# Stores and loads in alternating quarters, with a store semaphore for each quarter of a slot

## The chip, the cores and the metric

One core of a Trainium2 chip runs the kernel. The metric is the device time of one execution in microseconds (us), the median of the runs.

## What is computed

`x` is [2048, 64, 16, 16] in float32: 2048 samples of 64 channels, 16 x 16 pixels. It is group-normalised (32 groups of two channels, so over 512 values), padded by one pixel with a few border pixels copied from elsewhere, and run through three masked 4 x 4 convolutions with stride 2 (each mask keeps five taps). Their outputs go to three of the four parities of the output grid, are masked, and are added to x:

```
def _gn(v, G=32, eps=1e-5): ...            # (v - mean) / sqrt(var + eps) over each group
xp = jnp.pad(x, ((0, 0), (0, 0), (1, 1), (1, 1)))
xp = xp.at[:, :, DST_R, DST_C].set(xp[:, :, SRC_R, SRC_C])
up, left, right = (_conv(xp, w * mask, b) for each)
out[0::2, 0::2], out[1::2, 0::2], out[1::2, 1::2] = up, left, right
return x + out * OUT_MASK                  # xp is made from _gn(x)
```

## The kernel before

The samples are cut into 64 chunks of 32. A chunk is 2 MB: 128 partitions (two samples of 64 channels) by 16 pairs (`G`) by 256 pixels. It lives in one of eight slots (`SLOTS`) of the SBUF tensor `xs`, chunk k in slot k % 8, is normalised from there into `tn`, and has the convolution's results added in place, so that the slot is stored from where it was loaded.

The engines work as follows on chunk k. DVE takes the statistics of chunk k+1 (`bn`, L229, two waits on the load's two halves, `loaded[half][slot]`) between the small steps of chunk k (`moments`, `norms`), then normalises half of the pairs of chunk k (L277). ACT takes the root (L307), moves the four PSUM banks of chunk k-2 to `res` (`evacuate`, L336) and normalises the other half (L313). POOL adds `res` of chunk k-2 onto `xs` (`add`, L401, four banks, each raising `bank_added`) and copies the wrapped border pixels of chunk k (`wrap`, L411, five copies). PE does 240 matmuls a chunk (L459).

SP issues all large transfers, in the order written in its block. It first loads the weights, the four quarters of chunk 0 (L199) and chunks 1 to 6 in halves of 1 MB (L189). Then, for each chunk k and each half, it waits until the chunk's adds are done, issues the store of the half (L193), waits until both halves of chunk k-1, which has the slot of chunk k+7, are stored (L211), and issues the load of that half of chunk k+7 (`AHEAD` is 7):

```
for half in range(2):
    sp.wait_ge(bank_added, NB * (k + 1) if k < NCHUNK - 1 else NB * k + 4 + 2 * half)
    store(k, half)
    if n < NCHUNK:
        if n >= SLOTS:
            sp.wait_ge(stored[n % SLOTS], 32 * (n // SLOTS))
        load(n, half)
```

A slot has one semaphore for its two stores, and a transfer raises its semaphore by 16, so 32 a turn means both halves. The rows of a transfer are 1 KB in DRAM.

Of the kernel before, what the change touches and what calls it, by code (L numbers as in the profile page):

```python
# [16 lines left out]
G = 16  # L17
NCHUNK = B // (2 * G)
SLOTS = 8
# [38 lines left out]
NB = len(BANKS)  # L58
# [3 lines left out]


QUARTER = G // 4
HALF = (slice(0, G // 2), slice(G // 2, G))
AHEAD = 7


# [16 lines left out]
def view(tensor, at, dims, first=0, parts=P):  # L85

    full = tensor[:, ]
    row = full.ap[0][0]
    return bass.AP(full.tensor, full.offset + first * row + at, [[row, parts]] + [list(d) for d in dims])


def hex_conv(nc, x, w_up, b_up, w_left, b_left, w_right, b_right, out):
    ctx = ExitStack()
    with ctx:
        def sb(name, shape, dt):
            return ctx.enter_context(nc.sbuf_tensor(name, shape, dt))

        def sem(name):
            return ctx.enter_context(nc.semaphore(name))

        x_dram = x.rearrange("(n g h) c r q -> n (h c) g (r q)", g=G, h=2)
        out_dram = out.rearrange("(n g h) c r q -> n (h c) g (r q)", g=G, h=2)

        xs = sb("xs", [P, SLOTS, G * PIX], F32)
# [21 lines left out]
        def w_raw(t):  # L126
            at = C * 16 * W_AT[t][1]
            return tn[1][W_AT[t][0]:W_AT[t][0] + C, at:at + C * 16]
# [3 lines left out]
            return tn[1][W_AT[t][0]:W_AT[t][0] + C, at:at + C]  # L132

        loaded = [[sem(f"loaded{s}_{half}") for s in range(SLOTS)] for half in range(2)]
        stored = [sem(f"stored{s}") for s in range(SLOTS)]
        w_loaded = [sem(f"w_loaded{t}") for t in range(3)]
        b_loaded = sem("b_loaded")
        quarter = [sem(f"quarter{n}") for n in range(2)]
        cleared = sem("cleared")
        identity = sem("identity")  # L140
        edges_clear = sem("edges_clear")
# [12 lines left out]
        bank_added = sem("bank_added")  # L154
# [26 lines left out]

        @block.sync
        def _(sp):
            def part(dram, k, pairs):
                return dram[k][:, pairs], xs[:, k % SLOTS, :].rearrange("p (g q) -> p g q", g=G)[:, pairs]

            def load(k, half):
                frm, to = part(x_dram, k, HALF[half])
                sp.dma_start(to, frm).then_inc(loaded[half][k % SLOTS], 16)  # L189

            def store(k, half):
                to, frm = part(out_dram, k, HALF[half])
                sp.dma_start(to, frm).then_inc(stored[k % SLOTS], 16)  # L193

            for t, w in enumerate((w_up, w_left, w_right)):
                sp.dma_start(w_raw(t), w.rearrange("o c a b -> o (c a b)")).then_inc(w_loaded[t], 16)
            for n in range(4):
                frm, to = part(x_dram, 0, slice(QUARTER * n, QUARTER * (n + 1)))
                sp.dma_start(to, frm).then_inc((quarter[n // 2], loaded[n // 2][0])[n % 2], 16)  # L199
            for k in range(1, AHEAD):  # L200
                for half in range(2):
                    load(k, half)

            for k in range(NCHUNK):
                n = k + AHEAD
                for half in range(2):
                    sp.wait_ge(bank_added, NB * (k + 1) if k < NCHUNK - 1 else NB * k + 4 + 2 * half)
                    store(k, half)
                    if n < NCHUNK:
                        if n >= SLOTS:  # L210
                            sp.wait_ge(stored[n % SLOTS], 32 * (n // SLOTS))  # L211
                        load(n, half)
            for s in range(SLOTS):
                sp.wait_ge(stored[s], 32 * (NCHUNK // SLOTS))

        @block.vector
        def _(dve):
            def bn(k, u0, u1):

                if k >= NCHUNK:  # L220
                    return
                s = k % SLOTS
                if k and u0 in (0, G // 4):
                    dve.wait_ge(loaded[4 * u0 // G][s], 16 * (k // SLOTS + 1))
                if k and u0 == 0 and u1 == G // 2:
                    dve.wait_ge(loaded[1][s], 16 * (k // SLOTS + 1))
                for u in range(u0, u1):
                    both = view(xs, (s * G + 2 * u) * PIX, [(1, PIX), (PIX, 2)])
                    last = nc.vector.bn_stats(stats[:, k % 2, 2 * u:2 * u + 2].rearrange("p g a -> p (g a)"), both)  # L229
                if u1 == G // 2:  # L230
                    last.then_inc(bn_done, 1)

            def moments(k, ahead):

                done = STAT_OPS * k
                own = stats[:, k % 2]
                nc.vector.stream_shuffle(mate[:].rearrange("p g a -> p (g a)"), own.rearrange("p g a -> p (g a)"),  # L237
                                         [p ^ 1 for p in range(32)]).then_inc(stat_step, 1)
                bn(ahead, 0, 1)
                dve.wait_ge(stat_step, done + 1)  # L240
                nc.vector.tensor_tensor(gap[:], own[:, :, 1], mate[:, :, 1], ALU.subtract).then_inc(stat_step, 1)
                nc.vector.tensor_tensor(m2[:], own[:, :, 2], mate[:, :, 2], ALU.add).then_inc(stat_step, 1)  # L242
                nc.vector.tensor_tensor(msum[:], own[:, :, 1], mate[:, :, 1], ALU.add).then_inc(stat_step, 1)  # L243
                dve.wait_ge(stat_step, done + 2)
                nc.vector.scalar_tensor_tensor(gap2[:], gap[:], float(PIX // 2), gap[:],  # L245
                                               op0=ALU.mult, op1=ALU.mult).then_inc(stat_step, 1)
                bn(ahead, 1, 2)
                dve.wait_ge(stat_step, done + 5)

                nc.vector.scalar_tensor_tensor(var[:], gap2[:], EPS * GROUP, m2[:],  # L250
                                               op0=ALU.add, op1=ALU.add).then_inc(var_ready, 1)
                bn(ahead, 2, 4)

            def norms(k, ahead):

                done = STAT_OPS * k + 5
                dve.wait_ge(std_ready, k + 1)
                nc.vector.reciprocal(small[:, 0], std[:]).then_inc(stat_step, 1)  # L258
                bn(ahead, 4, 5)
                dve.wait_ge(stat_step, done + 1)  # L260
                nc.vector.scalar_tensor_tensor(small[:, 1], var[:], -0.5 / GROUP, small[:, 0],  # L261
                                               op0=ALU.mult, op1=ALU.mult).then_inc(stat_step, 1)
                bn(ahead, 5, 6)
                dve.wait_ge(stat_step, done + 2)
                nc.vector.tensor_tensor(small[:, 2], small[:, 1], small[:, 0], ALU.mult).then_inc(stat_step, 1)  # L265
                bn(ahead, 6, 7)
                dve.wait_ge(stat_step, done + 3)
                nc.vector.scalar_tensor_tensor(rstd[:], small[:, 2], 1.5, small[:, 0],  # L268
                                               op0=ALU.add, op1=ALU.mult).then_inc(stat_step, 1)
                bn(ahead, 7, 8)  # L270
                dve.wait_ge(stat_step, done + 4)
                nc.vector.scalar_tensor_tensor(nmr[:], msum[:], -0.5, rstd[:],  # L272
                                               op0=ALU.mult, op1=ALU.mult).then_inc(norm_ready, 1)

            def t_pairs(b, s, g0, g1):
                for g in range(g0, g1):
                    last = nc.vector.tensor_scalar(t_image(b, g), x_image(s, g), rstd[:, g:g + 1], nmr[:, g:g + 1],  # L277
                                                   ALU.mult, ALU.add)
                return last

            def normalise(k, pairs=GD):
                dve.wait_ge(norm_ready, k + 1)
                wait_t_free(dve, k)
                t_pairs(k % 2, k % SLOTS, 0, pairs).then_inc(t_dve, 1)

            for n in range(4):
                dve.wait_ge((quarter[n // 2], loaded[n // 2][0])[n % 2], 16)
                bn(0, QUARTER // 2 * n, QUARTER // 2 * (n + 1))
            dve.wait_ge(bn_done, 1)
            moments(0, NCHUNK)  # L290
            norms(0, NCHUNK)
            normalise(0, GD0)
            bn(1, 0, G // 2)
            dve.wait_ge(bn_done, 2)

            for k in range(1, NCHUNK):
                moments(k, k + 1)
                norms(k, k + 1)
                normalise(k)
                if k + 1 < NCHUNK:  # L300
                    dve.wait_ge(bn_done, k + 2)
# [210 lines left out]
```

## Time and profile before

| | |
|---|---|
| median of 3 runs | 740.97 us (740.41 to 741.33) |
| the profiled execution | 742.11 us, its span 740.3 us |
| busy | PE 655.8, DVE 613.8, ACT 574.8, POOL 473.9 us |
| bytes moved | 269.62 MB, mean 364 GB/s |
| transfers of x and out | 128 stores and 126 loads of 1 MB, 4 loads of 512 KB |
| issue to landing, median | 11.1 us for 1 MB, 8.4 us for 512 KB |

Busy time is that of an engine's instructions; issuing a DMA does not count. The page's time slices are tenths of busy time in 40 equal parts of the span. In a chain or a list of waits, SPq is SP's sequencer, which issues the DMAs. An issue that the queue cannot take yet lasts longer. Who is waited for is inferred, and where the engine named had long been done, it was another.

### The profile page before, as it was taken

What the parts mean: (1) busy time and instruction counts of PE and PEld (TensorE: products, weight loads), DVE (VectorE), ACT (ScalarE), POOL (GpSimd) and SP (SyncE); (2) the same over time, 40 slices, a digit from 0 to 9 for tenths busy, and PEclk for the clock granted to TensorE, in tenths of its full rate; (3) what the DMA queues carried; (4) which work ended last, traced back from release to release, by engine and by line L of the source; (5) the groups of instructions that cost most, each with busy time, mean ns of one, the idle gap of its engine ahead of it and who ended that gap; (6) DMA issues with size and microseconds to landing.
All of it is one profiled execution on the core that took longest, in us unless ns stands there. A gap on an engine that the chain in (4) does not pass through costs nothing.

```text
span 740.3 us, 36046 instructions
## 1 busy us (share of the span) xinstructions
PE 655.8 (89%) x15484; PEld 602.8 (81%) x15484; DVE 613.8 (83%) x1793; ACT 574.8 (78%) x1235; POOL 473.9 (64%) x1109
## 2 busy tenths in 40 slices
PE   1699999999999989889889898898898988989893
PEld 1589999999999888778788787787887878878883
DVE  4999999999999778788787787887977878878740
ACT  3488888988888787787877877878778778787782
POOL 1177777787776765756657657566576575665774
PEclk9989999999999999999999999999999999999997
DMA  8999999999999999999999999999999999999998
GB/s 262 349 362 384 384 380 373 367 367 374 374 356 366 366 367 370 365 379 368 366 369 367 374 370 367 374 365 362 379 361 375 362 366 376 365 365 374 378 352 286
DMA packets 267034, 269.62 MB, mean 364 GB/s; under 512 B 4656, under 2 KB 266800, under 8 KB 266992
## 3 DMA queue, kind: packets, MB, share of 16 engines
q1 hardware_dynamic: 266512, 269.24, 106.0%
q14 instruction: 38, 0.31, 0.1%
q10 hardware_dynamic: 480, 0.00, 0.0%
q8 instruction: 4, 0.07, 0.0%
HBM read 135.01 MB, written 134.22 MB: 364 GB/s over the span
## 4 chain that ended last, share of the span: by engine, by line
DMA 36%; DVE 31%; ACT 12%; POOL 10%; SPq 4%; issue 3%; PE 3%; POOLq 0%; ACTq 0%
DMA xs<-in_x 35%; DVE stats L229 17%; ACT tn L313 12%; DVE tn L277 7%; POOL xs L401 5%; POOL tn L411 4%; SPq L193 3%; PE bank L459 3%; DVE small L261 2%; DMA out<-xs 1%; DVE nmr L272 1%; DVE small L265 1%; DVE rstd L268 1%; DVE var L250 1%; DVE mate L237 0%
## 5 line engine op out<-in xcount | busy, mean ns | idle before, releaser
L459 PE MATMUL bank<-tn,wts 64*64 64x192 f32 (+1 forms) x15360 | 646.9, 325 | 0.0
L459 PEld LDWEIGHTS bank<-tn,wts 64*64 64x64 f32 x15360 | 593.4, 137 | 34.1
L229 DVE BATCH_NORM_STATS2 stats<-xs 128x6 f32<-128x512 f32 x512 | 350.4, 697 | 95.1 <-DMA xs<-in_x 95.1
L401 POOL TENSOR_TENSOR xs<-res,xs 128x192 f32<-128x192 f32 (+6 forms) x775 | 376.1, 530 | 7.7 <-ACT res L336 5.8
L313 ACT ACTIVATE tn<-xs,nmr,rstd 128x256 f32<-128x256 f32 x511 | 258.9, 592 | 78.7 <-DVE nmr L272 78.1
L336 ACT ACTIVATE res<-bank,bias 64x512 f32<-64x512 f32 (+5 forms) x640 | 302.1, 472 | 21.1 <-PE bank L459 10.9
L411 POOL COPY tn<-tn 128x128 f32<-128x128 f32 (+2 forms) x320 | 97.3, 362 | 242.2 <-ACT tn L313 242.2
L277 DVE TENSOR_SCALAR tn<-xs,rstd,nmr 128x256 f32<-128x256 f32 x513 | 181.5, 427 | 2.3
L470 PEld LDWEIGHTS bank<-blank 128*128 128x128 f16 x64 | 6.1, 96 | 82.5 <-ACT res L336 65.8
L470 PE MATMUL bank<-blank 128*128 128x2 f16 x64 | 11.2, 176 | 63.9 <-POOL tn L411 63.8
L307 ACT ACTIVATE std<-var 128x16 f32<-128x16 f32 x64 | 13.8, 216 | 49.7 <-DVE var L250 49.7
L261 DVE SCALAR_TENSOR_TENSOR small<-var,small 128x16 f32<-128x16 f32 x64 | 26.4, 412 | 0.1
L265 DVE TENSOR_TENSOR small<-small 128x16 f32<-128x16 f32 x64 | 19.6, 306 | 0.1
L250 DVE SCALAR_TENSOR_TENSOR var<-gap,m 128x16 f32<-128x16 f32 x64 | 19.5, 304 | 0.1
L268 DVE SCALAR_TENSOR_TENSOR rstd<-small 128x16 f32<-128x16 f32 x64 | 18.1, 283 | 0.1
L258 DVE RECIPROCAL small<-std 128x16 f32<-128x16 f32 x64 | 14.8, 232 | 1.0 <-ACT std L307 1.0
L272 DVE SCALAR_TENSOR_TENSOR nmr<-msum,rstd 128x16 f32<-128x16 f32 x64 | 13.7, 214 | 0.1
L237 DVE STREAM_SHUFFLE mate<-stats 128x48 f32<-128x48 f32 x64 | 13.0, 204 | 0.0
L439 PE MATMUL bank<-ident,tn 64*64 64x64 f32 x60 | 3.5, 316 | 8.6 <-ACT tn L177 8.6
L242 DVE TENSOR_TENSOR m<-stats,mate 128x16 f32<-128x16 f32 x64 | 11.1, 173 | 0.0
L243 DVE TENSOR_TENSOR msum<-stats,mate 128x16 f32<-128x16 f32 x64 | 11.0, 172 | 0.0
L245 DVE SCALAR_TENSOR_TENSOR gap<-gap 128x16 f32<-128x16 f32 x64 | 10.7, 167 | 0.0
(18 smaller groups left out, 24.1 us busy)
## 6 DMA issues: line engine op xcount, KB each, us to landing
out<-xs SPq DMA_DIRECT2D x128, 1024.0 KB, 11.1
xs<-in_x SPq DMA_DIRECT2D x126, 1024.0 KB, 11.1
xs<-in_x SPq DMA_DIRECT2D x4, 512.0 KB, 8.4
tn<-in_L_conv_w_up SPq DMA_DIRECT2D x1, 256.0 KB, 3.8
tn<-in_L_conv_w_left SPq DMA_DIRECT2D x1, 256.0 KB, 4.3
tn<-in_L_conv_w_right SPq DMA_DIRECT2D x1, 256.0 KB, 6.2
bias<-in_L_conv_b_up ACTq DMA_DIRECT2D x2, 0.2 KB, 4.5
bias<-in_L_conv_b_left ACTq DMA_DIRECT2D x2, 0.2 KB, 6.0
```

The source lines that it names most:

```text
L193: sp.dma_start(to, frm).then_inc(stored[k % SLOTS], 16)
L229: last = nc.vector.bn_stats(stats[:, k % 2, 2 * u:2 * u + 2].rearrange("p g a -> p (g a)"), both)
L250: nc.vector.scalar_tensor_tensor(var[:], gap2[:], EPS * GROUP, m2[:], op0=ALU.add, op1=ALU.add).then_inc(var_ready, 1)
L261: nc.vector.scalar_tensor_tensor(small[:, 1], var[:], -0.5 / GROUP, small[:, 0], op0=ALU.mult, op1=ALU.mult).then_inc(stat_step, 1)
L265: nc.vector.tensor_tensor(small[:, 2], small[:, 1], small[:, 0], ALU.mult).then_inc(stat_step, 1)
L268: nc.vector.scalar_tensor_tensor(rstd[:], small[:, 2], 1.5, small[:, 0], op0=ALU.add, op1=ALU.mult).then_inc(stat_step, 1)
L277: last = nc.vector.tensor_scalar(t_image(b, g), x_image(s, g), rstd[:, g:g + 1], nmr[:, g:g + 1], ALU.mult, ALU.add)
L313: last = nc.scalar.activation(t_image(k % 2, g), x_image(k % SLOTS, g), ACT.Identity, bias=nmr[:, g:g + 1], scale=rstd[:, g:g + 1])
L336: last = nc.scalar.activation(res[onto, BANK_AT[j] + at:BANK_AT[j] + at + cols], psum[NB * b + j][banks, at:at + cols], ACT.Identity, bias ...
L401: last = nc.gpsimd.tensor_tensor(onto, frm, onto, ALU.add)
L411: last = nc.gpsimd.tensor_copy(view(tn[b], dst, [(T_PAIR, G)] + [(d, n) for d, _, n in dims]), view(tn[b], src, [(T_PAIR, G)] + [(d, n) fo ...
L459: last = nc.tensor.matmul(psum[bank + j][to:to + C, at:at + cols], wts[first:first + C, NT * rect[0] + n, :], taps(b, rect, tap, first), s ...
```

## The change

SP's stores and loads go by quarters of four pairs (512 KB) in the order store, load, store, load. Each quarter q of a slot has a store semaphore of its own, `stored[q][slot]`, and the load of quarter q of chunk k+7 waits for the store of quarter q of chunk k-1 alone. Both quarters of a half raise the same load semaphore as before, so DVE waits for 32 where it waited for 16. Chunk 0 gets four semaphores for its four quarters (two were shared with `loaded`), so that slot 0's counts start one turn later. `PIECES` is 1: a quarter is one transfer.

```diff
-HALF = (slice(0, G // 2), slice(G // 2, G))
+NQ = 4
+PIECES = 1
...
-        stored = [sem(f"stored{s}") for s in range(SLOTS)]
+        stored = [[sem(f"stored{s}_{q}") for s in range(SLOTS)] for q in range(NQ)]
...
-            def load(k, half):
-                frm, to = part(x_dram, k, HALF[half])
-                sp.dma_start(to, frm).then_inc(loaded[half][k % SLOTS], 16)
-
-            def store(k, half):
-                to, frm = part(out_dram, k, HALF[half])
-                sp.dma_start(to, frm).then_inc(stored[k % SLOTS], 16)
+            def pieces(dram, k, q):
+                n = QUARTER // PIECES
+                for at in range(QUARTER * q, QUARTER * (q + 1), n):
+                    pairs = slice(at, at + n)
+                    yield dram[k][:, pairs], xs[:, k % SLOTS, :].rearrange("p (g q) -> p g q", g=G)[:, pairs]
+
+            def load(k, q):
+                for frm, to in pieces(x_dram, k, q):
+                    sp.dma_start(to, frm).then_inc(loaded[q // 2][k % SLOTS], 16)
+
+            def store(k, q):
+                for to, frm in pieces(out_dram, k, q):
+                    sp.dma_start(to, frm).then_inc(stored[q][k % SLOTS], 16)
+
+            def wait_added(k, q):
+                sp.wait_ge(bank_added, NB * (k + 1) if k < NCHUNK - 1 else NB * k + 4 + 2 * (q // 2))
+
+            def wait_stored(k, q):
+
+                if k >= SLOTS:
+                    sp.wait_ge(stored[q][k % SLOTS], 16 * PIECES * (k // SLOTS))
...
             for k in range(NCHUNK):
                 n = k + AHEAD
-                for half in range(2):
-                    sp.wait_ge(bank_added, NB * (k + 1) if k < NCHUNK - 1 else NB * k + 4 + 2 * half)
-                    store(k, half)
+                for q in range(NQ):
+                    wait_added(k, q)
+                    store(k, q)
                     if n < NCHUNK:
-                        if n >= SLOTS:
-                            sp.wait_ge(stored[n % SLOTS], 32 * (n // SLOTS))
-                        load(n, half)
+                        wait_stored(n, q)
+                        load(n, q)
...
+            def wait_loaded(k, half):
+
+                turns = k // SLOTS + (k % SLOTS > 0)
+                dve.wait_ge(loaded[half][k % SLOTS], 16 * 2 * PIECES * turns)
+
...
-                    dve.wait_ge(loaded[4 * u0 // G][s], 16 * (k // SLOTS + 1))
+                    wait_loaded(k, 4 * u0 // G)
```

## Rows read from the trace of the kernel before

**Rows 1.** The page: busy time, DMA busy tenths, bytes and mean rate.

```profile
PE 655.8 (89%) x15484; PEld 602.8 (81%) x15484; DVE 613.8 (83%) x1793; ACT 574.8 (78%) x1235; POOL 473.9 (64%) x1109
...
DMA  8999999999999999999999999999999999999998
...
DMA packets 267034, 269.62 MB, mean 364 GB/s; under 512 B 4656, under 2 KB 266800, under 8 KB 266992
```

**Rows 2.** Windows by stage: us, busy by engine, PEclk, DMA share, GB/s.

```profile
9.00:13.50 4.50, 3.09 (x59) 2.90 (x55) 3.52 (x6) 2.85 (x12) 1.04 (x3) 1.00 1.11 350
16.00:44.00 28.00, 17.97 (x320) 15.54 (x324) 27.39 (x80) 15.22 (x33) 8.88 (x22) 0.88 1.10 349
54.00:94.00 40.00, 40.00 (x963) 36.91 (x958) 39.85 (x109) 35.03 (x76) 29.73 (x68) 1.00 1.09 384
94.00:690.00 596.00, 548.12 (x13030) 504.38 (x13026) 511.00 (x1508) 479.80 (x1025) 394.84 (x918) 1.00 1.07 369
706.00:731.00 25.00, 21.27 (x514) 19.36 (x504) 6.19 (x13) 18.23 (x40) 18.93 (x42) 1.00 1.02 342
```

**Rows 3.** Waits on SP and DVE, 300 to 641 us.

```profile
SPq L189 <- DMA out<-xs: 92.0, 30, 3.3
SPq L193 <- POOL xs L401: 56.8, 60, 1.7
...
DVE stats L229 <- DMA xs<-in_x: 61.2, 30, 2.4
```

**Rows 4.** Chain of waits in the middle, in order of time.

```profile
300.55 11.15 DMA xs<-in_x
...
311.72 0.71 DVE stats L229
...
323.31 11.14 DMA xs<-in_x
```

**Rows 5.** Stores issued and POOL's copies up to 309.5 us.

```profile
L193 SPq DMA_DIRECT2D out<-xs x48: 1563/2517/3530, 43.1 to 309.4; - x48
...
L411 POOL COPY tn<-tn x140: 236/414/472, 21.4 to 309.1; 128x128 f32<-128x128 f32 x84, 128x64 f32<-128x64 f32 x28, 128x32 f32<-128x32 f32 x28
```

**Rows 6.** SP's issues in order of time, middle.

```profile
298.07 2.43 SPq L193 DMA_DIRECT2D out<-xs  x1
...
303.35 2.63 SPq L193 DMA_DIRECT2D out<-xs  x1
309.02 0.37 SPq L189 DMA_DIRECT2D xs<-in_x  x1
309.43 2.28 SPq L193 DMA_DIRECT2D out<-xs  x1
...
320.41 0.37 SPq L189 DMA_DIRECT2D xs<-in_x  x1
```

**Rows 7.** Windows of one microsecond around the end of the wait.

```profile
309.00:310.00 1.00, 0.53 (x9) 0.47 (x13) 0.64 (x2) 0.96 (x3) 1.00 (x3) 1.00 1.09 388
310.00:311.00 1.00, 1.00 (x23) 0.81 (x18) 0.00 (x0) 0.97 (x2) 1.00 (x3) 1.00 0.99 331
311.00:312.00 1.00, 1.00 (x24) 0.85 (x16) 0.28 (x1) 0.95 (x4) 1.00 (x3) 1.00 1.00 282
312.00:315.00 3.00, 3.00 (x68) 2.86 (x64) 3.00 (x8) 1.25 (x4) 3.00 (x8) 1.00 1.04 350
```

**Rows 8.** Waits of SP, 60 to 94 us.

```profile
SPq L189 <- DMA out<-xs: 8.9, 3, 3.1
```

**Rows 9.** Start: the first half load's issue and the first statistics.

```profile
6.15 2.13 SPq L189 DMA_DIRECT2D xs<-in_x  x1
...
9.49 1.31 DVE L229 BATCH_NORM_STATS2 stats<-xs 128x6 f32<-128x512 f32 x2 [9.49 <-DMA xs<-in_x]
```

**Rows 10.** Chain of waits at the end.

```profile
687.70 11.15 DMA xs<-in_x
...
708.21 9.98 PE bank L459 x184
```

More of the change, by code:

```diff
@@ L134, in hex_conv @@
         loaded = [[sem(f"loaded{s}_{half}") for s in range(SLOTS)] for half in range(2)]
-        stored = [sem(f"stored{s}") for s in range(SLOTS)]
+        stored = [[sem(f"stored{s}_{q}") for s in range(SLOTS)] for q in range(NQ)]
         w_loaded = [sem(f"w_loaded{t}") for t in range(3)]
         b_loaded = sem("b_loaded")
-        quarter = [sem(f"quarter{n}") for n in range(2)]
+        quarter = [sem(f"quarter{q}") for q in range(NQ)]
         cleared = sem("cleared")
@@ L183, in _ @@
         def _(sp):
-            def part(dram, k, pairs):
-                return dram[k][:, pairs], xs[:, k % SLOTS, :].rearrange("p (g q) -> p g q", g=G)[:, pairs]
-            def load(k, half):
-                frm, to = part(x_dram, k, HALF[half])
-                sp.dma_start(to, frm).then_inc(loaded[half][k % SLOTS], 16)
-            def store(k, half):
-                to, frm = part(out_dram, k, HALF[half])
-                sp.dma_start(to, frm).then_inc(stored[k % SLOTS], 16)
+            def pieces(dram, k, q):
[3 more added lines that the diff above has]
+                    yield dram[k][:, pairs], xs[:, k % SLOTS, :].rearrange("p (g q) -> p g q", g=G)[:, pairs]
@@ L195, in _ @@
             for t, w in enumerate((w_up, w_left, w_right)):
                 sp.dma_start(w_raw(t), w.rearrange("o c a b -> o (c a b)")).then_inc(w_loaded[t], 16)
-            for n in range(4):
-                frm, to = part(x_dram, 0, slice(QUARTER * n, QUARTER * (n + 1)))
-                sp.dma_start(to, frm).then_inc((quarter[n // 2], loaded[n // 2][0])[n % 2], 16)
+            for q in range(NQ):
+                for frm, to in pieces(x_dram, 0, q):
+                    sp.dma_start(to, frm).then_inc(quarter[q], 16)
@@ L200, in _ @@
             for k in range(1, AHEAD):
-                for half in range(2):
-                    load(k, half)
+                for q in range(NQ):
+                    load(k, q)
             for k in range(NCHUNK):
                 n = k + AHEAD
-                for half in range(2):
-                    sp.wait_ge(bank_added, NB * (k + 1) if k < NCHUNK - 1 else NB * k + 4 + 2 * half)
-                    store(k, half)
+                for q in range(NQ):
+                    wait_added(k, q)
+                    store(k, q)
@@ L209, in _ @@
                     if n < NCHUNK:
-                        if n >= SLOTS:
-                            sp.wait_ge(stored[n % SLOTS], 32 * (n // SLOTS))
-                        load(n, half)
+                        wait_stored(n, q)
+                        load(n, q)
             for s in range(SLOTS):
-                sp.wait_ge(stored[s], 32 * (NCHUNK // SLOTS))
+                for q in range(NQ):
+                    sp.wait_ge(stored[q][s], 16 * PIECES * (NCHUNK // SLOTS))
         @block.vector
@@ L223, in bn @@
                 if k and u0 in (0, G // 4):
-                    dve.wait_ge(loaded[4 * u0 // G][s], 16 * (k // SLOTS + 1))
+                    wait_loaded(k, 4 * u0 // G)
                 if k and u0 == 0 and u1 == G // 2:
-                    dve.wait_ge(loaded[1][s], 16 * (k // SLOTS + 1))
+                    wait_loaded(k, 1)
                 for u in range(u0, u1):
@@ L284, in normalise @@
                 t_pairs(k % 2, k % SLOTS, 0, pairs).then_inc(t_dve, 1)
-            for n in range(4):
-                dve.wait_ge((quarter[n // 2], loaded[n // 2][0])[n % 2], 16)
-                bn(0, QUARTER // 2 * n, QUARTER // 2 * (n + 1))
+            for q in range(NQ):
+                dve.wait_ge(quarter[q], 16 * PIECES)
+                bn(0, QUARTER // 2 * q, QUARTER // 2 * (q + 1))
             dve.wait_ge(bn_done, 1)
```

## Prediction, made before the change was run

> **What bounds the kernel now.** I read the page's summary first. No compute engine is full: PE is busy for 89% of the span, DVE 83%, ACT 78%, POOL 64%, while the DMA row stands at 9 in nearly all 40 slices and the rate is near 370 GB/s from end to end [rows 1]. 269.6 MB have to be moved and the change moves the same bytes, so what counts is the rate and the two ends.
>
> The windows by stage say what rates there are [rows 2]. The opening is loads alone, at 349 to 350 GB/s. When stores alternate with loads the rate is first 384 (54 to 94 us). From 94 us to 690, where the loads' issues end, it is 369. The stores alone at the end run at 342. The 596 us from 94 to 690 moved 596 by 369 = 219.9 MB. One chunk is 2.10 MB in and 2.10 MB out: 4.19 MB take 11.37 us at 369 and 10.92 us at 384.
>
> That the transfers set the pace in this stretch is shown by the waits: between 300 and 641 us DVE waits 61.2 us in 30 stops for a load [rows 3], 2.0 us a chunk, and the chain of waits goes from the landing of a load through statistics, ACT's normalising, POOL's copies and adds to SP again, period 11.4 us [rows 4]. Early on DVE has no such wait (in the list of waits for 60 to 94 us it is not named). One link of the chain has to be distrusted, the step from POOL's add to SP's store. By 309.5 us SP has issued 48 stores, so the last is chunk 23, second half; POOL by then has made 140 copies, five a chunk, so chunks 0 to 27 are wrapped and the adds up to chunk 25, which stand before the wrap of 27, are done [rows 5]. The add that store 24 needs is long past; SP's 56.8 us "for POOL" [rows 3] is time in which the queue took no more.
>
> Now SP's own timeline [rows 6]. A 1 MB issue lasts 2.3 to 2.8 us in three of four cases: it is held until there is room. The store issued at 309.43 ends at 311.71, and the load issued at 300.55, three transfers ahead of it, landed at 311.70 [rows 4]. So about 3 MB are in flight when SP is free to push. Once a chunk it is not: load 30, first half, goes into slot 6 and waits for both halves of chunk 22, whose second half was issued at 298.07, only three transfers earlier. SP stands from 305.98 to 309.02, and 30 such waits cost SP 92.0 us in the window [rows 3], 3.1 us each. After the wait the issue takes only 0.37 us: there was room all along. In those 3 us the stock shrinks from 3 MB to 2 MB.
>
> By the microsecond, the rate is 388 when the wait ends, then 331 and 282 in the two microseconds from 310 to 312, then a mean of 350 for three more [rows 7]. Against 384 this lacks 53+102+3 by 34 = 257 KB, 0.67 us of this chunk, of which the first two microseconds hold 155 KB, 60%.
>
> My reading: a transfer is spread over 16 engines that do not run in step. SP's wait is for the slowest of the 16; the fastest have by then used up more of their share, run out, and have to wait for the next load's descriptors. The dip is theirs.
>
> **The change part by part.** *The wait.* Load quarter q of chunk n waits for store quarter q of chunk n-8. Eight quarter transfers lie between the two, so 4 MB have been issued behind the quarter waited for. With 3 MB in flight it has landed when SP comes to ask, by some 1 MB, 2.7 us. Each wait of 3.1 us becomes about nothing, and SP is held by a full queue alone. Bounds: nothing gained (the dip has another cause) or the whole distance from 369 to 384. The latter: 219.9 MB at 384 take 572.7 us instead of 596, 23.3 us less. I take the part of the dip that stands directly behind the wait, 60%: 14.0 us. The other 40% begins 3 us after the wait ended, and I can't tie it to it.
>
> Against my reading stands one set of rows: from 60 to 94 us the same waits were there, three of them, 8.9 us together [rows 8], and the rate was 384 all the same [rows 2]. If engines drift apart slowly, this fits (they have not yet drifted far); if not, it speaks for the rival below.
>
> *Does the queue count bytes or transfers?* If transfers, quarters would halve the stock. At the start four quarter loads and one half were all issued by 8.28 us (6.15 and 2.13), and the first statistics, which need the first quarter only, begin at 9.49 [rows 9]: five transfers were outstanding, 3 MB of them. So it goes by amount, and six quarters will be outstanding.
>
> *Number of issues.* SP issues eight transfers a chunk for four: 8 by 0.37 us, the free issue [rows 6], are 3.0 us of 11.4. Hidden behind a full queue. Were none of it hidden, the 254 added transfers (512 for 258) would cost 254 by 0.37 = 94 us; the other bound is nothing. The nearest row for the transfer itself: the window with the quarter loads has 350 GB/s, that with half loads 349 [rows 2]. I take nothing.
>
> The Trainium skill ("DMA: Bandwidth & Descriptors", Measured and Rules for kernel authors) speaks against the change: at least 1 MiB a DMA, since about 2.0 us are fixed in each. Taken as serial time that would be some 500 us for 254 more. The trace does not agree: 1 MB passes in 11.39/4 = 2.85 us [rows 6], fixed part included, so it overlaps in the queue.
>
> *Landing and DVE.* The order of bytes is S L S L in quarters where it was in halves; the first half of a load is complete after the same 2 MB of the chunk, the second after 4. DVE's waits are two as before, each on a count of two quarters. No gain, no loss. The adds that gate the stores are long done, so four checks of them for two cost nothing.
>
> *The ends.* The opening moves the same loads. After the last load lands at 698.85 the chain runs on through two convolutions, one of them the 9.98 us shown, to the last adds [rows 10]; 41.5 us from landing to the end of the span, all of it unchanged. If loads come sooner DVE is still the one who waits: PE needs 9.98 us a chunk [rows 10], under 10.92.
>
> Sum against the span: 740.3 - 14.0 = 726.3. The profiled execution took 742.1, the runs' median is 741.0, 0.7 above the span, so 727.0 us is my forecast for the median. The likeliest case alone goes from 718 (all of the 23.3 us) to 738 (a fifth of the 14.0).
>
> **The rivals.** *Same.* The slowest of the 16 engines never runs dry: at 309.02 it still has two transfers, 2 MB. If its own pace is 11.37 us a chunk, refilling the fast ones earlier makes them lead further and nothing ends sooner: 741, within 739.5 to 742.5. For it: the clean rate in spite of the same wait at 60 to 94 us. Against: the dip follows the wait's end. The Trainium skill ("DMA: Bandwidth & Descriptors", Latency and other measured facts) says that some DMA engines are usually slower than the others; no view here names the engines.
>
> *Slower by turns.* The dip is the price of going from load to store and back, not of the wait. Then twice the turns give twice the loss: 741.0 + 23.3 = 764. It decides if the after trace has two dips a chunk. For it: the dip sits where a load ends (311.70) and a store follows. Against: the same turns from 54 to 94 us at 384 GB/s, and three of four turns of a chunk without a dip. A milder form is a small cost for each added transfer: 0.01 to 0.05 us by 254 is 3 to 13 us, 744 to 754.
>
> *The change does not remove the wait.* If less room is used than I think or stores land late, the quarter's wait remains for a part of its 3.1 us. The time is then between this forecast and 741, and counts with them.
>
> **How the numbers follow.** Faster by the wait, 0.47; same by the slowest engine, 0.27; slower by turns or by transfers, 0.26. Below 718, for a rate above 384, I leave 0.05 and take 714 as the end; above 747 stands about 0.14. The range is 714 to 747; it takes in all of the same case and the milder half of the slower one. The bound of same is 0.2%, 1.5 us, about what runs of this kernel (740.4 to 741.3) can tell.
>
> **What would show it.** Right: SP's waits for stores at the load line gone or under 0.5 us; issues held about 1.3 us each by room; no microsecond under 340 in the middle; windows after 94 us at 377 or more; DVE's wait a chunk under 2 us with a period near 11.1. Wrong: SP's waits gone, but windows still at 369 (same), or dips at more places and 350 to 360 (turns); an opening under 345 GB/s would show a cost for each transfer.

## The result, and the profile after

The changed kernel takes 735.39 us (median of 4 runs, 734.90 to 735.63) against 740.88 us before (740.41 to 741.33): ratio 0.9925, 95% interval 0.9908 to 0.9942. It is 5.5 us faster, where 14 were forecast. The profiled execution's span is 733.1 us where it was 740.3; these two lie 7.2 us apart, more than the medians, because the profiled execution before (742.11 us) took longer than all four runs of that median, and that of the changed kernel (734.90 us) is its fastest.

The page of the changed kernel: busy time; DMA's tenths and GB/s in 40 slices of 18.3 us; packets; DMA issues with their median time to landing.

```profile
PE 655.4 (89%) x15484; PEld 602.6 (82%) x15484; DVE 617.0 (84%) x1793; ACT 575.0 (78%) x1235; POOL 473.3 (65%) x1109
...
DMA  8999999999999999999999999999999999999998
GB/s 265 348 360 384 384 384 379 373 375 372 370 370 373 371 375 372 365 373 374 371 381 381 368 376 377 371 361 376 378 375 377 375 375 376 372 362 374 383 353 285
DMA packets 271100, 269.65 MB, mean 368 GB/s; under 512 B 8720, under 2 KB 270864, under 8 KB 271056
...
xs<-in_x SPq DMA_DIRECT2D x256, 512.0 KB, 8.0
out<-xs SPq DMA_DIRECT2D x256, 512.0 KB, 8.3
```

The same bytes go at 368 GB/s in the mean for 364 [rows 1]. 384 lasts for three slices, about 55 to 110 us, and then the rate sinks to some 374, as it sank to 369 before. A quarter lands 8.0 us after its issue: at 374 GB/s that is 3.0 MB, six quarters, as the prediction had it.

Windows by stage of the changed kernel, columns as in [rows 2]:

```profile
9.00:13.50 4.50, 2.31 (x44) 2.12 (x41) 3.38 (x6) 2.10 (x8) 1.04 (x3) 1.00 1.11 349
16.00:44.00 28.00, 18.52 (x340) 15.97 (x344) 27.39 (x81) 15.10 (x33) 8.88 (x22) 0.94 1.10 348
54.00:94.00 40.00, 40.00 (x964) 36.82 (x960) 39.85 (x112) 35.31 (x77) 30.32 (x68) 1.00 1.09 384
94.00:690.00 596.00, 553.37 (x13181) 509.48 (x13177) 521.21 (x1528) 484.49 (x1035) 396.73 (x925) 1.00 1.08 374
```

The opening is the same (349 and 348 for 350 and 349), 54 to 94 us too. All of the gain lies in the long stretch: 5 GB/s more over 596 us are 3.0 MB, 8.0 us at 374, about the 7.2 us between the two spans (the rates are rounded to whole GB/s).

Waits of the changed kernel on SP and DVE, 300 to 641 us (total us, times, longest):

```profile
SPq L197 <- POOL xs L418: 48.5, 60, 1.8
...
DVE stats L246 <- DMA xs<-in_x: 53.9, 30, 2.3
```

SP's line for stores, 92.0 us before [rows 3], is gone. DVE's wait for loads fell from 61.2 us to 53.9 only, 1.8 us a chunk: the loads are still what it waits for.

SP's issues in order of time:

```profile
299.81 1.73 SPq L197 DMA_DIRECT2D out<-xs  x1
301.58 1.37 SPq L193 DMA_DIRECT2D xs<-in_x  x1
303.00 1.29 SPq L197 DMA_DIRECT2D out<-xs  x1
...
309.75 1.24 SPq L193 DMA_DIRECT2D xs<-in_x  x1
311.03 1.71 SPq L197 DMA_DIRECT2D out<-xs  x1
```

Eight issues a chunk, each held 1.2 to 1.7 us by room. The same issue comes back after 11.22 us (299.81 to 311.03) for 11.39 before.

Low microseconds are left, as this window shows:

```profile
319.00:320.00 1.00, 1.00 (x17) 0.84 (x21) 0.13 (x1) 0.96 (x3) 1.00 (x2) 1.00 0.94 298
```

Of 360 windows of one microsecond from 300 us on, 18 are under 340 GB/s; before it was 47.

Chain of waits at the end:

```profile
683.53 8.08 DMA xs<-in_x
...
701.00 9.97 PE bank L476 x188
...
724.33 2.54 POOL xs L418 x10
```

The last load of the chain lands at 691.61, before at 698.85 [rows 10]: 7.2 us earlier, which is the whole difference of the spans. From there to the end it is 41.5 us in both.

So SP's waits for stores went as forecast, and the rate rose by 5 GB/s only. Either the rest of the gain was lost to something new, or the wait had never held the rate.

### The profile page after: what moved, and what is told of

It is laid out like the page before. It is cut to its first block, busy times and chain, and to the rows that moved or that the text cites. A ratio compares the mean times of both kernels' runs of the same rounds, so it can differ in the third digit from the quotient of the medians.

```text
span 733.1 us, 36312 instructions
## 1 busy us (share of the span) xinstructions
PE 655.4 (89%) x15484; PEld 602.6 (82%) x15484; DVE 617.0 (84%) x1793; ACT 575.0 (78%) x1235; POOL 473.3 (65%) x1109
## 4 chain that ended last, share of the span: by engine, by line
DVE 36%; DMA 25%; POOL 18%; ACT 12%; issue 3%; PE 3%; SPq 2%; POOLq 0%
DMA xs<-in_x 25%; DVE stats L246 19%; POOL xs L418 13%; ACT tn L330 12%; DVE tn L294 8%; POOL tn L428 5%; PE bank L476 3%; DVE small L278 2%; SPq L197 2%; DVE small L282 2%; DVE rstd L285 2%; DVE nmr L289 1%; DVE mate L254 1%; DVE var L267 0%; DVE small L275 0%
## 5 line engine op out<-in xcount | busy, mean ns | idle before, releaser
L282 DVE TENSOR_TENSOR small<-small 128x16 f32<-128x16 f32 x64 | 24.8, 388 | 0.1
L285 DVE SCALAR_TENSOR_TENSOR rstd<-small 128x16 f32<-128x16 f32 x64 | 21.2, 331 | 0.1
L267 DVE SCALAR_TENSOR_TENSOR var<-gap,m 128x16 f32<-128x16 f32 x64 | 17.6, 275 | 0.1
L289 DVE SCALAR_TENSOR_TENSOR nmr<-msum,rstd 128x16 f32<-128x16 f32 x64 | 12.7, 199 | 0.1
```

## Experiments

Each kernel is told with the median of its runs and its ratio to the kernel before on the same chip, with its 95% interval. The copies beside one engine are single runs, but for two runs each of the halves and the short loop beside PE. Differences in us between two changed kernels are taken from medians that can come from different chips, on which the kernel before had medians from 740.51 to 741.69 us, so they are good to about 1 us. GB/s are those of the window from 94 to 650 us of each trace. In this window the kernel before has 369 and the changed one 374.

### The wait alone

Kernel before, still halves of 1 MB, each half with its own store semaphore, so that four transfers have been issued behind the store that a load waits for, and not two:

```diff
-        stored = [sem(f"stored{s}") for s in range(SLOTS)]
+        stored = [[sem(f"stored{s}_{half}") for s in range(SLOTS)] for half in range(2)]
...
-                            sp.wait_ge(stored[n % SLOTS], 32 * (n // SLOTS))
+                            sp.wait_ge(stored[half][n % SLOTS], 16 * (n // SLOTS))
```

> The kernel before with one thing of the change: each half of a slot has a store semaphore of its own, so the load of a half waits for a store issued a whole chunk earlier. Transfers stay at 1 MB. Theory (the wait was what cost): SP's waits for stores are gone and the time is that of the changed kernel, 735 us (733.5 to 737). Rival (the finer alternation brought the gain): 741 (739.5 to 742.5).

741.36 us against 741.69, ratio 0.9998 (0.9989 to 1.0007). Its waits on SP and DVE from 300 to 641 us, and its windows of one microsecond:

```profile
SPq L193 <- POOL xs L402: 69.3, 59, 2.1
...
DVE stats L230 <- DMA xs<-in_x: 61.3, 30, 2.4
```

```profile
309.00:310.00 1.00, 1.00 (x22) 0.77 (x18) 0.00 (x0) 0.95 (x3) 1.00 (x2) 1.00 1.01 294
310.00:311.00 1.00, 1.00 (x24) 0.85 (x20) 0.43 (x1) 0.97 (x3) 1.00 (x3) 1.00 1.09 384
```

The wait is gone and nothing has become faster: 370 GB/s, and DVE waits 61.3 us as it did before (61.2). Dips are there as well, 294 GB/s in one microsecond, with no wait of SP ahead of it; of 360 microseconds from 300 us on, 36 are under 340 GB/s where it was 47, and the bytes missing against 384 GB/s are the same, 5.4 MB in both. This fells the theory of the prediction: what the dips cost was not made by the wait.

The changed kernel with one store semaphore for a slot, as before, so that load quarter q waits for all four store quarters of the chunk:

```diff
-                    sp.wait_ge(stored[q][k % SLOTS], 16 * PIECES * (k // SLOTS))
+                    sp.wait_ge(stored[k % SLOTS], 16 * NQ * PIECES * (k // SLOTS))
```

> The changed kernel with one store semaphore for a slot, so a load quarter waits for all four store quarters, the last of them issued 1.5 MB before. Theory (the wait costs, by the stock it leaves): the wait leaves 1 MB instead of 2 MB of the 3 MB, more than the engines' spread of some 3.5 us can bear, so it is worse than the kernel before: 755 us (745 to 800). Rival (granularity alone): 735.

748.08 us, ratio 1.0104 (1.0081 to 1.0127); 367 GB/s, and only 369 from 54 to 94 us. Its waits on SP, 300 to 641 us:

```profile
SPq L193 <- DMA out<-xs: 113.7, 30, 4.2
```

3.8 us a chunk, for a store with one quarter load and one quarter store behind it: 1 MB of stock is left, where the wait of before left 2 MB. With 2 MB left, in halves, the wait costs nothing; with 1 MB left, in quarters, it costs 748.1 - 735.4 = 12.7 us. The issue behind this costly wait takes 0.37 us too (at 300.75 us), just as behind the free one [rows 6], so a short issue tells of room in the queue and not of a loss. Own semaphores are therefore needed for quarters, but are no gain in themselves. The 748.08 lie in the range that was expected, 745 to 800.

### The transfers alone

SP's block alone, all computing left out (the output is x): once with the changed kernel's quarters, once with the halves and the wait of before.

```diff
             def wait_added(k, q):
-                sp.wait_ge(bank_added, NB * (k + 1) if k < NCHUNK - 1 else NB * k + 4 + 2 * (q // 2))
+                if k == 0:
+                    sp.wait_ge(quarter[q], 16 * PIECES)
+                else:
+                    sp.wait_ge(loaded[q // 2][k % SLOTS], 32 * PIECES * (k // SLOTS + (k % SLOTS > 0)))
```

> Leaves out all computation: SP's block of the changed kernel alone, each store waiting for its load, output is x. If the transfers themselves are held to 374 GB/s in the middle, the rate in the windows stays at 374 and the span is some 705 to 715 us (the tail's 41 us from last landing to the end shrinks). If the computation or its instruction fetches slow them, the rate is 384 throughout and the time is under 705.

> Leaves out all computation: SP's block of the kernel before alone, output is x. If the 3 us wait per chunk costs by itself, it is 5 us or more above the copy in quarters. If the wait costs only where one DMA engine already lags (as the landings in the trace suggest for the kernel before), and nothing makes one lag here, it is within 1.5 us of it.

Quarters 714.06 us (0.9627), halves 712.08 us (0.9601). Windows of the copy in quarters (POOL busy, PEclk, DMA share, GB/s):

```profile
54.00:94.00 40.00, 0.00 (x0) 1.00 1.09 385
94.00:650.00 556.00, 0.00 (x0) 1.00 1.09 385
```

Windows of the copy in halves, and its waits on SP, 300 to 641 us:

```profile
54.00:94.00 40.00, 0.00 (x0) 1.00 1.09 385
94.00:650.00 556.00, 0.00 (x0) 1.00 1.09 386
```

```profile
SPq L189 <- DMA out<-xs: 80.0, 31, 2.7
```

Three things follow. 254 more transfers cost 2.0 us, 8 ns each. The wait of 2.6 us a chunk stands in the copy as well, at 386 GB/s: it costs nothing. And the transfers by themselves keep 385 to 386 until 650 us; the 369 to 374 come from the computing beside them. It is the rate that decides this: the time that was expected beside it, under 705 us, was too low. The question was then which engine.

### The copy with one engine beside it

The copy in quarters, with one engine working on scratch: statistics and scalings on DVE, activations on ACT, adds and copies on POOL, or on PE 33 turns of a loop over the kernel's own convolutions of two chunks, which wait for nothing:

```diff
+            with pe.Fori(0, 33) as i:
                 for b in range(2):
-                    pe.wait_ge(t_ready, 2 * i + b + 1)
                     convolve(2 * i + b, b)
```

> Leaves out the computation: the copy in quarters with DVE beside it alone, 62 rounds of the kernel's statistics and scalings on scratch tiles, waiting for no transfer. Copy alone: 385 GB/s in every window from 54 us on, span 712 us. If DVE's reads and writes of SBUF slow the transfers, 375 to 380 GB/s and 718 to 730 us; if not, 385 and 712 to 714.

> Leaves out the computation: the copy in quarters with ACT beside it alone, on scratch tiles. If ACT slows the transfers, 375 to 380 GB/s; if not, 385 and a span of 712 to 714 us.

> Leaves out the computation: the copy in quarters with POOL's strided adds beside it alone, on scratch tiles. If POOL slows the transfers, 375 to 380 GB/s; if not, 385 and 712 to 714 us.

> Leaves out the computation: the copy in quarters with PE's loop of 240 float32 matmuls a chunk beside it alone, on scratch tiles, not waiting for anything. My first suspicion, since PE reads SBUF without a break: 370 to 378 GB/s and 722 to 735 us. If PE does not disturb the transfers: 385 and 712 to 714 us.

| beside the copy | us | GB/s 94 to 650 | engine busy in these 556 us | the same engine in the kernel before |
|---|---|---|---|---|
| nothing | 714.06 | 385 | | |
| POOL | 714.62 | 385 | 278 | 368 |
| ACT | 715.40 | 384 | 469 | 448 |
| DVE | 718.36 | 382 | 377 | 479 |
| PE | 732.79 | 373 | 556 | 513 |

DVE's and POOL's work ended early. While it lasted the rate was 381 GB/s beside DVE (94 to 480 us) and 385 beside POOL (94 to 400 us). The first row comes from another chip than the others, which have one run each.

Windows with PE beside (PE, PEld, POOL busy, PEclk, DMA share, GB/s):

```profile
54.00:94.00 40.00, 40.00 (x1010) 38.41 (x1006) 0.00 (x0) 1.00 1.09 385
94.00:650.00 556.00, 556.00 (x13867) 534.73 (x13863) 0.00 (x0) 1.00 1.08 373
650.00:690.00 40.00, 11.42 (x299) 10.56 (x289) 0.00 (x0) 0.68 1.07 373
```

PE alone reproduces the figure of the kernel: 385 from 54 to 94 us, then 373. PE's loop moves no data of the transfers and works on other tiles than theirs.

Then the same PE loop beside the copy in halves with the wait of before:

> Leaves out the computation: SP's block of the kernel before (1 MB transfers, the 3 us wait) with PE's long loop beside it. If PE is the whole of the disturbance and the order of transfers decides how much of it is felt, this stands some 6 us above the copy in quarters with PE: 737 to 740. If not, 730 to 733.

732.07 us (0.9881), 373 GB/s, with SP's wait for stores in place (87.9 us from 300 to 641 us): beside PE alone, halves with the wait and quarters without it don't differ.

### Columns or instructions

Three other PE loops beside the copy in quarters: a turn of 24 matmuls of 192 columns, where the loop above has 240; of 68 matmuls of 512 columns; of 240 of 64 columns. A matmul of the program leaves two records (the 240 a chunk of the kernel count records).

```diff
+            with pe.Fori(0, 44) as i:
+                for n in range(120):
+                    for first in (0, C):
+                        nc.tensor.matmul(psum[n % 8][first:first + C, 0:64], wts[first:first + C, n % NTAP, :],
+                                         tn[n % 2][first:first + C, 128 * (n % 16):128 * (n % 16) + 64], start=True, stop=True,
```

> Leaves out the computation: the copy in quarters with PE beside it as in the run with PE's long loop, as many float32 matmuls of 192 columns, but in a loop of 24 matmuls instead of 480. If PE's SBUF reads disturb the transfers, 372 to 376 GB/s and 727 to 735 us again; if it is the reading in of PE's long loop of instructions, 385 GB/s and 714 us.

> Leaves out the computation: the copy in quarters with PE looping over 68 matmuls of 512 columns, as many columns an iteration as the kernel's 240 matmuls, with less than a third of the instructions. If the columns read from SBUF disturb the transfers: 372 to 376 GB/s as before with PE's long loop. If the instructions of the loop do: 381 to 384.

> Leaves out the computation: the copy in quarters with PE looping over 240 matmuls of 64 columns: the kernel's number of instructions an iteration, less than half of its columns. If the instructions disturb the transfers: 374 GB/s or less. If the columns do: 380 or more.

The loops of short turns and of wide matmuls last longer than the copy (3114.88 and 1072.27 us in all), so only their windows are compared; the narrow one takes 747.04 us. The 400 us from 150 to 550 of the short, the wide and the narrow loop in this order, one fence each:

```profile
150.00:550.00 400.00, 400.00 (x4100) 322.38 (x4098) 0.00 (x0) 1.00 1.09 385
```

```profile
150.00:550.00 400.00, 400.00 (x1868) 140.28 (x1866) 0.00 (x0) 1.00 1.09 385
```

```profile
150.00:550.00 400.00, 400.00 (x13722) 400.00 (x13718) 0.00 (x0) 1.00 1.06 363
```

With two records a matmul, wide is 1868 / 2 by 512 / 400 = 1196 columns a microsecond and narrow 13722 / 2 by 64 / 400 = 1098. At nearly the same columns, seven times the instructions take the rate from 385 to 363. By records in 400 us: 1868 and 4100 cost nothing, 9965 (the loop above) 13 GB/s, 13722 22. How many columns PE computes is not what slows the transfers, but how many instructions it runs in a microsecond. The granted clock is full in all of these windows. Each record of a matmul has one of a weight load beside it, so whether matmuls or weight loads do it these loops can't tell. (The short loop was meant to have fewer instructions in its body at the same pace; its records came every 98 ns for every 40 in the loop above, so it tells of the pace and nothing of the size of the body.)

The control in the whole kernel: before, with the wait as it was, but only one of the five taps of each convolution computed, which leaves out four fifths of PE's matmuls.

```diff
+                        if n < NT - 1:
+                            continue
```

> The kernel before with one of the five taps of each convolution, so a fifth of PE's matmuls; the sums of the other taps are left out. Transfers, order and the 3 us wait are unchanged. If PE's instructions slow a DMA engine in the whole kernel as in the copy: 382 to 385 GB/s in the windows from 94 us on, and about 710 to 718 us (also a shorter tail, by some 16 us of convolutions). If the wait for the stores is what costs: the rate stays at 369 to 372.

721.64 us, ratio 0.9734 (0.9714 to 0.9753). Windows (columns as in [rows 2]) and SP's waits for stores, 300 to 641 us:

```profile
54.00:94.00 40.00, 13.45 (x196) 11.06 (x196) 39.86 (x113) 35.27 (x76) 29.30 (x68) 0.55 1.09 384
94.00:650.00 556.00, 174.32 (x2548) 143.76 (x2548) 494.48 (x1452) 460.27 (x986) 376.53 (x884) 0.56 1.08 381
```

```profile
SPq L189 <- DMA out<-xs: 85.8, 31, 3.5
```

The wait stands at 85.8 us and the rate is 381 all the same. Of the 17 GB/s between the kernel before (369) and the copy in halves (386), leaving out four fifths of PE's matmuls gives back 12; of the 5 left DVE alone would account for some 4 (385 to 381 beside the copy), if such losses add up, which no run shows. This control takes away instructions and columns together, and PE's granted clock is 0.56 in it, so that it is instructions rests on the loops above. Rate and time are a little short of what was expected (382 to 385, 710 to 718 us): the last load lands at 678.9 us, 41.0 before the end, so the tail did not shorten as the expectation had it. This is where most of the missing rate is; the wait has no part in it, and the change brings back 5 of the 17.

### What in the change brings the 5.5 us

The changed kernel with its quarters and their own semaphores, but in the order store, store, load, load:

```diff
-                for q in range(NQ):
-                    wait_added(k, q)
-                    store(k, q)
+                for half in range(2):
+                    for q in (2 * half, 2 * half + 1):
+                        wait_added(k, q)
+                        store(k, q)
...
-                        wait_stored(n, q)
-                        load(n, q)
+                        for q in (2 * half, 2 * half + 1):
+                            wait_stored(n, q)
+                            load(n, q)
```

> The changed kernel with its 512 KB transfers and own semaphores, but in the order store, store, load, load, so the direction turns as in the kernel before. The copies alone say that 254 more transfers cost 2.0 us (714.06 against 712.08). If the finer alternation is what gains: 741.4 + 2 = 743 (741.5 to 745). If smaller transfers or the finer waits gain: 735 to 737.

744.91 us, ratio 1.0056 (1.0042 to 1.0070); 368 GB/s. The same transfers of the same size in another order: 9.5 us more than the changed kernel. So cutting the halves up costs 744.9 - 741.4 = 3.5 us in the full kernel (4.3 by the ratios), and letting the direction turn every 512 KB for every 1 MB gives back 9.5 (9.7 by the ratios); together they are the gain. SP waits here for POOL alone, as in the changed kernel.

Finer: eighths, 256 KB, alternating, each with its own semaphore; and quarters of two pieces of 256 KB each (`PIECES = 2`), turning every 512 KB.

> The changed kernel in eighths: 256 KB transfers alternate, each eighth of a slot with its own store semaphore. 512 more transfers cost some 4 us. If the finer alternation is what gains, and another halving gives as much again as the last (8 us before its cost of 2), 731 to 734; if the gain is used up, 739. If alternation gains nothing, 739 too.

> The changed kernel with PIECES = 2: each quarter goes as two transfers of 256 KB one behind the other, so the direction turns every 512 KB as in the changed kernel. 512 more transfers at 8 ns (from the copies) are 4 us. If only the length of a run in one direction and the number of transfers count: 735.4 + 4 = 739.5 (738 to 741), near the 740.4 of the alternating eighths. If small transfers have a gain of their own: 736 or less.

Eighths 740.43 us (0.9994, 0.9985 to 1.0003), 371 GB/s, where 731 to 734 or 739 was expected: the gain is lost again. Two pieces 747.14 us (1.0076, 1.0050 to 1.0102), 366 GB/s, where 738 to 741 was expected. At the same turns, 256 more transfers of each kind cost 11.8 us, 23 ns each, three times their price in the copy. Against that, turning every 256 KB instead of every 512 (eighths against two pieces) gives 6.7. Size and turns pull against each other, and 512 KB alternating was the best of what ran.

### Two queues

Halves with own semaphores; SP issues the loads, ACT the stores (of chunk k-3 behind its normalising of chunk k, of the last three at the end):

```diff
+            def store(k):
+                for half in range(2):
+                    act.wait_ge(bank_added, NB * (k + 1) if k < NCHUNK - 1 else NB * k + 4 + 2 * half)
+                    act.dma_start(out_dram[k][:, HALF[half]],
...
+                if k >= 3:
+                    store(k - 3)
```

> Halves with own semaphores, but ACT issues the stores (of chunk k-3 behind its normalising of chunk k) and SP only the loads, so stores and loads stand in two queues and mix by the packet, with 1 MB transfers. If what the quarters gain is finer mixing of the directions, this gains it without the 2 us of the added transfers, and more: 725 to 733. If a lagging DMA engine alone sets the pace, whatever the order, 736 to 742. Danger: an issue that has to wait for room holds ACT; then above 745.

737.69 us, ratio 0.9944 (0.9928 to 0.9961), where 725 to 733 was expected: within 2.3 us of the changed kernel, but for another reason. Windows (columns as in [rows 2]) and waits from 94 to 650 us:

```profile
94.00:650.00 556.00, 516.51 (x12271) 476.13 (x12265) 535.50 (x1422) 452.78 (x963) 384.74 (x861) 1.00 1.08 382
...
680.00:735.00 55.00, 39.91 (x959) 36.91 (x951) 23.76 (x64) 35.25 (x75) 35.27 (x82) 0.90 0.76 253
```

```profile
ACT std L296 <- issue: 81.1, 41, 3.0
```

With loads and stores on two queues the rate is 382 with all of PE's instructions beside it. DVE no longer waits for loads in the middle; it is busy for 535.50 of 556 us and bounds the kernel, with ACT late by its issues (81.1 us in 41 stops). DVE's own instructions have become longer: the 1793 of the run take 671.0 us for 613.8 before; why is not shown. The stores fall behind, and the last 55 us run at 253 GB/s. The Trainium skill ("Trainium Kernel Development and Optimization", Key Constraints) says that DMAs of all queues run on the same 16 DMA engines, and that issuing from several engines at once only saves issue time. The rate here doesn't agree with it: 382 GB/s for 370 with the same halves and semaphores on one queue, where issuing was held by room and not short of time.

The same with POOL as the issuer:

> Loads from SP, stores of 1 MB from POOL behind its copies of each chunk. If descriptors from POOL cost it little: 385 GB/s until the loads end and 716 to 725 us. If POOL pays several us for a store (1024 rows of 1 KB each) it becomes the bound, since it has about 4 us free a chunk: above 745 us.

797.57 us, ratio 1.0764 (1.0721 to 1.0808); 353 GB/s, and DVE's busy time is 752.8 us for 613.8 before, with the same 1793 instructions. It was expected above 745 us if POOL became the bound; it is DVE that did, with 95% of the span busy for POOL's 74%. No gain there.

## Why the prediction was right or wrong, by its steps

**What bounds the kernel** was right: transfers set the pace in the stretch from 94 us; the gain is there alone, and DVE still waits for loads after the change. What sets the transfers' own rate there, PE's instructions for the most part, stood in no rival.

**The wait goes** was right, and all that it said of SP came: no wait for stores, issues of 1.2 to 1.7 us, six quarters in flight, so that the queue goes by amount.

**The step that failed** is "I take the part of the dip that stands directly behind the wait, 60%: 14.0 us", and the reading under it, that the fastest DMA engines had run dry. The wait taken away alone brought nothing (741.36 against 741.69), with a dip to 294 GB/s still there; the copy in halves has the wait (80.0 us) and no microsecond under 340; and the kernel with one tap reaches 381 with the wait in place. What stood behind the wait in time did not come from it. So the term of 14.0 us is nothing for the wait, and the 5.5 us that were measured come from a term that the sum did not have, the order of the transfers, less the price of cutting them. That the time moved the way that was forecast is luck. The prediction had evidence against its term: the same wait at 384 GB/s from 60 to 94 us [rows 8], and its own count of 2 MB left at the wait's end, which at 369 GB/s are 5.7 us of transfers. The fastest DMA engine is 3.6 us ahead of the slowest (below), so by this estimate it had some 2 us of work left and had not run dry.

**Its signs** came in part: SP's waits for stores gone, issues held 1.2 to 1.7 us, DVE's wait 1.8 us a chunk with a period of 11.22. The two on the rate did not: 374 GB/s where 377 was asked, and 18 of 360 microseconds under 340.

**The rival "same"** was right on the wait: taking it away lets the fast engines lead further, and nothing ends sooner. The landing records bear this out. Each transfer lands in 16 parts, one for each DMA engine by the prediction's reading; the records don't name the engines. The table has the mean time from the first to the last part of a store, 300 to 640 us, counted from the landings in the traces.

| | first to last part, us | GB/s |
|---|---|---|
| before | 3.6 | 369 |
| the wait alone removed | 4.0 | 370 |
| changed | 3.5 | 374 |
| changed, order store, store, load, load | 3.7 | 368 |
| copy in halves, in quarters | 1.4, 1.9 | 386, 385 |
| copy beside the wide, the short loop | 1.7, 2.4 | 385, 385 |
| copy beside PE's convolutions, the narrow loop | 3.7, 4.0 | 373, 363 |
| before with one tap | 3.0 | 381 |

In this table all that ran under 375 GB/s has a lag of 3.5 us or more, and all that ran above 380 one of 3.0 or less. In the changed kernel with one store semaphore for a slot, whose wait leaves 1 MB, the lag is 1.0 us at 367 GB/s: there the wait itself holds the fast engines back. This fits a slowest engine that sets the pace once the others are as far ahead as the queue lets them; it doesn't show it, as the records don't tell whether it is always the same engine. Why the rival's time (741) was still wrong: it left out that the order of the transfers changes the rate.

**The rival "slower by turns"** had the sign wrong. More turns of direction at 512 KB gave 9.5 us, and no slice of 18.3 us of the changed kernel between 94 and 690 us shows the 350 to 360 of that rival. Its milder form, a small price for each added transfer, is there in the full kernel: 3.5 to 4.3 us for 254, within its 3 to 13, and was outweighed.

**Transfers at nothing**: 2.0 us in the copy, 3.5 in the kernel, where nothing was taken. A small term, but of the size of the result. The fixed cost that the prediction weighed and set aside would as serial time have been some 500 us; 8 ns each is what the copies show.

**The ends and DVE's landing order** at nothing were right: 41.5 us from the last landing to the end, as forecast, and 349 and 348 GB/s in the opening.

**What stays open.** Why the alternation in 512 KB raises the rate in the full kernel and not beside PE alone (halves 732.07, quarters 732.79) is not shown. So is the way in which PE's instructions reach the transfers. The Trainium skill ("Runtime: NRT & Kernel Launch", Instruction fetch mechanics) says that PE's instructions stand in a buffer of 128 KiB, refilled by DMA in blocks of 16 KiB; a stream of instructions would then be traffic on a DMA engine. The traces show only four such reads on PE's queue in the whole run (16 KB each, 0.07 MB), the last of them at 163 us in the copy beside PE's convolutions, with the loop run 33 times and the rate low to the end of it, so they don't confirm it; whether every read is recorded is not known. All runs here were profiled, so that the writing of one record for each PE instruction may have a part in it too.

## What to carry to other kernels

A wait that a queue's stock covers costs nothing: count what is left in flight against the lag between the first and the last part of a landing (5.7 us against 3.6 here). A short issue behind the wait decides nothing: it was 0.37 us both where the wait cost nothing and where it cost 12.7. Before a low rate is blamed on SP's waits, run the transfers alone, then beside one engine at a time: here they made 385 GB/s alone and the wait was worth nothing, while the order store, load in 512 KB was worth 9.5 us. Cutting transfers finer has a price of its own (8 ns each alone, 14 to 23 ns in this kernel), so try one size at a time.

## What the runs showed of the hardware that was not expected

- PE's instructions (matmuls with their weight loads) slow the core's transfers, and its columns don't: 385 GB/s up to 4100 records in 400 us, 373 at 9965, 363 at 13722, one trace each.
- The loss sets in late. In the copy beside PE's convolutions the lag between the parts of a store is 1.7 us until about 100 us and reaches 3.6 by 140; the rate is still 380 or more until 140 us and sinks then. The kernel before sinks from about 95 us, the changed one from about 120.
- In the copy in quarters this lag stands still but for four steps of 0.5 to 0.6 us, at 108, 283, 457 and 632 us, and there stand SP's four reads of 8 KB of instructions. Beside the wide matmuls the first three of the same reads leave it at 1.7 us.
- Loads on SP's queue and stores on ACT's ran at 382 GB/s where one queue gave 366 to 374 with the same work beside it, and around 300 us issues on ACT stood for 5.2 and 5.8 us.
- Stores issued by POOL cost DVE 139 us of busy time for the same instructions, stores issued by ACT 57 us; why is not shown.
